# A third PSUM bank for the first pass of the attention, in the units that have bank 7 to spare

## The chip, the cores and the metric

The kernel runs on one core of a Trainium2 chip. The metric is the time of one execution on the device in microseconds (us). The core's engines are TensorE (PE in the profile; its weight loads are PEld), VectorE (DVE), ScalarE (ACT), GpSimd (POOL) and SyncE (SP, which issues most DMAs). They run their own instruction streams in order and wait for each other by semaphores. Matmuls write to PSUM, which has eight banks of 512 float32 in each of 128 partitions.

## What is computed

Two things are added to the input `x` (2 rows of 1024 tokens, 128 features), both from its layer norm: a transformer of four layers, and a mixture of experts (8 experts, 2 for each token) on all 2048 tokens. What matters here is the attention of the four layers: 16 heads of 8 features, causal, with ALiBi.

```python
def mha(x, mask, Wi, bi, Wo, bo):
    ...
    scores = jnp.einsum('bhqd,bhkd->bhqk', q, k) / math.sqrt(HD)
    scores = scores + mask[None]
    attn = jax.nn.softmax(scores, axis=-1)
    out = jnp.einsum('bhqk,bhkd->bhqd', attn, v)
    out = out.transpose(0, 2, 1, 3).reshape(B, T, D)
    return out @ Wo.T + bo
...
for i in range(L):
    xn = layer_norm(x, ln1_w[i], ln1_b[i])
    x = x + mha(xn, mask, in_proj_w[i], in_proj_b[i], out_proj_w[i], out_proj_b[i])
    xn = layer_norm(x, ln2_w[i], ln2_b[i])
    h = jax.nn.gelu(xn @ ffn1_w[i].T + ffn1_b[i], approximate=False)
    x = x + (h @ ffn2_w[i].T + ffn2_b[i])
return layer_norm(x, final_w, final_b)
```

## The kernel before

**Units and phases.** The attention of one row in one layer is cut into four units of four heads. Four units are a phase; a phase handles the attention of one row while projections, FFN and experts of the other row are worked in between. There are eight phases, 32 units: phase "first" (units 0 to 3), then three times "odd" and "even" in a loop over the layers (units 4 to 27, two jumps back), then "last" (units 28 to 31). The loop's body is written once and run three times; all other code is written out.

**Two passes.** The softmax needs each query's maximum. The first pass (`p1_step` on TensorE, `maximum` on VectorE) forms the scores of unit U + 1, 40 steps of up to 512 columns, and takes their row maxima. It has banks 5 and 6 of PSUM in turn: step k writes bank `5 + k % 2` and so waits until the maximum of step k - 2 is taken (`s_p1m`). The steps run over eight query tiles; after step 11 (query tiles 0 to 3) and after step 39 VectorE reduces the maxima to `negm`, one half of the queries each. GpSimd splits `negm` in three bf16 parts (`max_parts`, lines 601 to 608), TensorE turns them (`turn`, line 879) into bank 7, ScalarE copies them out (`turn_out`, line 766, counted by `s_taken`), and DMAs put them into the query operand. The second pass of unit U (`p2_pair`, line 984) then forms scores with the maximum subtracted, ScalarE takes the exponential (`exps`, line 797) from banks 0 to 3, and `p2_values` (line 1002) multiplies with the values into bank 4. A pair of step c waits for the exponential of step c - 2.

**Order.** Nothing is scheduled by a tool: each engine's order is written out by a table, `PLANS`. A unit has 24 slots (one `p2_pair` each) and 48 half slots; `pace` says how many first-pass steps are issued in each half slot; `contents` says in which slot a piece of other work is issued that goes through bank 7, the one bank for all of it: turns of maxima, layer norm transposes, projections (q, k, v), FFN pieces (h, y), the attention's output projection. Such a piece waits until the piece before it is out of the bank (`taken`), so all are numbered in one order (`base + n`).

**Units without other work.** In six units `contents` has nothing but turns: the first and third of "first" (units 0 and 2), the third of "even" (10, 18 and 26) and the third of "last" (30). There bank 7 stands empty between its two or three turns.

Of the kernel before, what the change touches and what calls it, by code (L numbers as in the profile page):

```python
# [33 lines left out]
ALU = mybir.AluOpType  # L34
ACT = mybir.ActivationFunctionType
AXX = mybir.AxisListType.X
# [3 lines left out]
P = 128  # L40
# [6 lines left out]
ROWS = 64  # L47
# [10 lines left out]
def first_pass():  # L58

    steps = []  # L60
    for i in range(TB):
        for c in range(1 + i // 4):
# [7 lines left out]
P1N = len(P1_STEPS)  # L70
P1L = sum(i < TB // 2 for i, *_ in P1_STEPS)
HALVES = 48
PLANS = {
    "first": dict(
        pace=("011111011111011111011111011111011101021111011111",
              "011111011111011112011110011111010111111111011021",
              "011111011111011112001111011111011111101111101111",
              "011101111001111100013101000043011111110111101111"),
        contents=(
# [62 lines left out]
def kind_of(b, f, q):  # L142

    return "first" if f is None else "last" if q is None else ("even", "odd")[b]


def steps_at(b, f, q, j, k):

    if j == 3 and q is None:
        return ()  # L150
    pace = [int(n) for n in PLANS[kind_of(b, f, q)]["pace"][j]]
    return tuple(range(sum(pace[:k]), sum(pace[:k + 1])))


P2_JOBS = [(qh, kt, max(512 * qh, P * kt), 512 * (qh + 1) - max(512 * qh, P * kt))
# [3 lines left out]
SLOTS = 2 * JOBN  # L159
# [41 lines left out]
def chunks_of(b, f, q):  # L201

    if f is None:
        return (3,)
    if q is None:
        return (0, 1)
    return (0, 1, 2, 3) if b == 1 else (0, 1, 3)
# [16 lines left out]
def build(nc, x, cA, rA, cB, moe1, moe2, router_w, rb, fin, ident, identb, iota, m1, m2, route, kcon, qcon, out):  # L224
    with ExitStack() as ctx:
# [642 lines left out]
        def _(pe):  # L868
# [84 lines left out]
                                         wA[:, 2 * D:3 * D], start=True, stop=True)  # L953
                last.then_inc(S["s_full"], 1)

            def p1_step(U, par, kb, nth, k, first=False):
                i, j, c, n, heads = P1_STEPS[k]
                if k == 0:
                    pe.wait_ge(c_ldl[par], 32 * (nth + 1))
                if k == P1L:  # L960
                    pe.wait_ge(c_ldr[par], 32 * (nth + 1))
                if k >= 2 or not first:
                    pe.wait_ge(S["s_p1m"], P1N * U + k - 1)
                r = slice(ROWS * j, ROWS * j + ROWS)
                diagonal = 512 * c + n == P * (i + 1)
                for e, a in enumerate(heads):
                    last = pe.matmul(PS[:, 5 + k % 2, n * e:n * e + n], Qop[r, par, a, P * i:P * i + P],  # L967
                                     Kop[r, kb, a, 512 * c:512 * c + n], start=True, stop=not diagonal)
                    if diagonal:
                        for side in range(2):  # L970
                            at = n * e + n - P + ROWS * side
                            last = pe.matmul(PS[:, 5 + k % 2, at:at + ROWS], mk1[r, side, :], idb[r, r],  # L972
                                             start=False, stop=side == 1)
                last.then_inc(S["s_p1"], 1)

# [31 lines left out]
            def phase(p, b, f, q, base, contents):  # L1007

                row = 1 - b
                g0 = gelus_before(b, f)  # L1010
                done = chunks_of(b, f, q)
                for j in range(PH):
                    U, par, nth = PH * p + j, j % 2, 2 * p + j // 2
                    for s in range(SLOTS):
                        for k in steps_at(b, f, q, j, 2 * s):
                            p1_step(U + 1, 1 - par, (j + 1) % 4, nth + par, k)
                        p2_pair(U, par, j, nth, s)
                        for n, (spots, kind, which) in enumerate(contents):
                            if SLOTS * j + s in spots:
                                if kind[:4] == "turn" and which == 1:  # L1020
                                    turn(base + n, U, par, 1)
                                if kind[:4] == "turn" and which == 0:
# [15 lines left out]
                                        if spots[t] == SLOTS * j + s:  # L1038
                                            y_piece(base + n, which, g0 + done.index(which), group_of(which, b, f), t)
                        for k in steps_at(b, f, q, j, 2 * s + 1):  # L1040
                            p1_step(U + 1, 1 - par, (j + 1) % 4, nth + par, k)
                        if s == 0 and not (f is None and j == 0):
                            p2_values(U - 1, 1 - par, JOBN - 1)
                        if s % 2 == 1 and s >= 3:
# [55 lines left out]
        def _(dve):  # L1100
# [109 lines left out]
                    dve.tensor_tensor(o, o, other, op).then_inc(S["s_fin"], 1)  # L1210
                    dve.wait_ge(S["s_fin"], 3 * (2 * row + c) + k + 1)

            def maximum(U, par, k):
                i, j, c, n, heads = P1_STEPS[k]
                dve.wait_ge(S["s_p1"], P1N * U + k + 1)
                dve.tensor_reduce(mx[:, par, i, 2 * heads[0] + j:2 * heads[-1] + j + 1:2, c],  # L1216
                                  PS[:, 5 + k % 2, 0:n * len(heads)].rearrange("p (h n) -> p h n", n=n), AXX, ALU.max)\
                    .then_inc(S["s_p1m"], 1)
                if k == P1L - 1 or k == P1N - 1:

                    tiles = slice(0, 4) if k == P1L - 1 else slice(4, 8)
                    dve.wait_ge(S["s_p1m"], P1N * U + k + 1)
                    dve.tensor_reduce(negm[:, par, tiles, :], mx[:, par, tiles, :, :], AXX, ALU.max, negate=True)\  # L1223
                        .then_inc(S["s_negm"], 1)
# [16 lines left out]
            def phase(p, b, f, q, base, contents):  # L1241
                row = 1 - b
                at = PLANS[kind_of(b, f, q)]
                for now in range(4 * HALVES):
                    j, k = now // HALVES, now % HALVES
                    U, par = PH * p + j, j % 2
                    for step in steps_at(b, f, q, j, k):
                        maximum(U + 1, 1 - par, step)
                    for n, (_, kind, which, away) in enumerate(at["contents"]):
                        if away == now and not (kind == "h" and CHUNKS[which[0]][0] == "X"):  # L1250
                            out_of_bank(base + n, kind, which, group_of(which, b, f) if kind == "y" else 0, 4 * p, b, row)
# [231 lines left out]
```

## Time and profile before

| what | value |
|---|---|
| median of 3 runs | 1548.06 us (1546.43 to 1549.83) |
| the profiled execution | 1548.17 us |
| its span in the profile | 1546.4 us |
| TensorE busy | 1272.3 us, 82% of the span |
| VectorE busy | 997.0 us, 64% |
| ScalarE busy | 873.0 us, 56% |
| GpSimd busy | 379.2 us, 25% |
| mean granted TensorE clock | 0.921 of full |

The span is the time from the first to the last instruction of the program in the profile; the execution's own time is a little longer. "Busy" is the time in which an engine has an instruction of its own under way. Matmuls are pipelined and their ends are modelled, so a busy TensorE is not one at its peak. All times below are counted from the start of the span.

### The profile page before, as it was taken

The page shows a single profiled execution, that of the slowest core. Times are in us where ns is not written, and L with a number is a line of the kernel's source. Part 1 is how long each engine was busy: PE and PEld are TensorE (multiplying, and loading weights), DVE is VectorE, ACT ScalarE, POOL GpSimd, SP SyncE. Part 2 cuts the span into 40 slices and gives each one's busy share as a digit, 9 for nine tenths or more (in the row PEclk, how much of TensorE's full clock was granted, in tenths as well). Part 3 has the DMA queues.
Part 4 walks back from the last instruction along what each step waited for, and adds up shares of the span by engine and source line. Part 5 has one row for each costly group of instructions (what it writes and reads, how often), then busy time and mean ns, then how long its engine had stood idle before and what let it go on. Part 6 is the DMA issues. An engine that isn't in the chain of part 4 may idle for free.

```text
span 1546.4 us, 35310 instructions
## 1 busy us (share of the span) xinstructions
PE 1272.3 (82%) x12316; PEld 647.1 (42%) x12316; DVE 997.0 (64%) x2120; ACT 873.0 (56%) x1107; POOL 379.2 (25%) x569
## 2 busy tenths in 40 slices
PE   3688788899888887889888897889988898976854
PEld 2333344345444443444444443444544444433323
DVE  5787666666666775666665776657666676745724
ACT  2056556666566664656655665566565666653740
POOL 4044503132031201222122110312203210424501
PEclk9589889999999998999998999999998999988986
DMA  8212414123230312313232131303313041201010
GB/s 247 65 45 86 173 38 128 31 73 116 73 117 19 117 50 65 111 33 115 80 103 66 59 107 54 112 18 114 108 58 97 20 140 36 88 30 48 18 48 15
DMA packets 108919, 120.64 MB, mean 78 GB/s; under 512 B 12097, under 2 KB 95169, under 8 KB 108737
## 3 DMA queue, kind: packets, MB, share of 16 engines
q1 hardware_dynamic: 100288, 90.38, 18.7%
q0 software_dynamic: 8448, 27.88, 6.0%
q8 instruction: 109, 1.79, 0.5%
q14 instruction: 74, 0.60, 0.1%
HBM read 78.63 MB, written 40.89 MB: 77 GB/s over the span
## 4 chain that ended last, share of the span: by engine, by line
PE 52%; DVE 15%; issue 14%; POOL 10%; ACT 6%; DMA 1%; POOLq 0%; DVEq 0%; ACTq 0%; SPq 0%
PE PS L1002 13%; PE PS L967 12%; DVE mx L1216 10%; PE PS L984 5%; PE PS L924 4%; PE PS L927 3%; PE PS L907 3%; PE PS L911 3%; ACT PR L797 2%; POOL xs L614 2%; POOL both L641 2%; PE PS L948 2%; PE PS L972 2%; PE PS L990 2%; PE PS L952 1%
## 5 line engine op out<-in xcount | busy, mean ns | idle before, releaser
L1216 DVE TENSOR_REDUCE mx<-PS 128x1 f32<-128x512 f32 (+3 forms) x1280 | 768.3, 633 | 351.2 <-PE PS L972 231.2
L797 ACT ACTIVATE PR<-PS 128x1024 f32<-128x1024 f32 (+3 forms) x768 | 607.4, 810 | 499.2 <-PE PS L990 311.4
L967 PE MATMUL PS<-Kop,Qop 64*128 64x512 bf16 (+3 forms) x1536 | 438.4, 346 | 140.1 <-DVE mx L1216 135.8
L984 PE MATMUL PS<-Qop,Kop 64*128 64x512 bf16 (+3 forms) x1536 | 349.0, 338 | 16.3 <-ACT PR L797 8.4
L1002 PE MATMUL PS<-PR,vbuf 128*32 128x512 f32 (+3 forms) x3072 | 342.4, 519 | 0.6 <-ACT PR L797 0.4
L967 PEld LDWEIGHTS PS<-Kop,Qop 64*128 64x128 bf16 x1536 | 130.9, 94 | 467.8 <-DVE mx L1216 371.4
L972 PE MATMUL PS<-idb,mk 64*128 64x64 bf16 x2048 | 192.0, 195 | 0.0
L972 PEld LDWEIGHTS PS<-idb,mk 64*128 64x128 bf16 x2048 | 163.4, 98 | 45.1 <-issue 7.2
L990 PE MATMUL PS<-idb,mk 64*128 64x64 bf16 x2048 | 168.3, 194 | 4.7 <-issue 4.7
L601 POOL CAST mp<-negm 128x16 bf16<-128x16 f32 x64 | 14.9, 234 | 555.2 <-DVE negm L1223 555.2
L990 PEld LDWEIGHTS PS<-idb,mk 64*128 64x128 bf16 x2048 | 136.3, 97 | 33.7 <-issue 8.3
L984 PEld LDWEIGHTS PS<-Qop,Kop 64*128 64x128 bf16 x1536 | 106.0, 95 | 104.7 <-ACT PR L797 58.0
L572 POOL TENSOR_TENSOR rstd<-ve,mhalf 128x4 f32<-128x4 f32 x40 | 41.1, 1027 | 240.7 <-DVE ve L1118 240.4
L1002 PEld LDWEIGHTS PS<-PR,vbuf 128*32 128x32 f32 x3072 | 61.6, 109 | 64.9 <-issue 34.6
L907 PE MATMUL PS<-xnT,wF 128*128 128x512 f32 x128 | 76.0, 687 | 11.9 <-ACT xnT L757 9.3
L924 PE MATMUL PS<-wF,hb 128*128 128x128 f32 x512 | 73.2, 294 | 4.5 <-ACT hb L779 2.9
L924 PEld LDWEIGHTS PS<-wF,hb 128*128 128x128 f32 x512 | 64.1, 200 | 13.3 <-issue 6.6
L577 POOL TENSOR_TENSOR x<-x,parts 128x1024 f32<-128x1024 f32 x16 | 34.1, 2128 | 131.1 <-ACT parts L784 131.1
L779 ACT ACTIVATE hb<-hb 128x2048 f32<-128x2048 f32 x26 | 49.7, 1910 | 18.9 <-DVE hb L1138 12.5
L927 PE MATMUL PS<-w2G,hb 128*128 128x128 f32 x320 | 54.0, 322 | 0.4 <-issue 0.4
L590 POOL TENSOR_TENSOR xr<-xr,wR 128x512 f32<-128x512 f32 x28 | 35.6, 1271 | 76.4 <-DVE xc L1130 76.4
L766 ACT ACTIVATE mrow<-PS 12x512 bf16<-12x512 bf16 x64 | 36.8, 575 | 27.5 <-PE PS L879 27.0
(104 smaller groups left out, 1117.3 us busy)
## 6 DMA issues: line engine op xcount, KB each, us to landing
Qop<-qst SPq DMA_DIRECT2D x64, 256.0 KB, 2.8
Kop<-kst SPq DMA_DIRECT2D x64, 256.0 KB, 3.3
kst<-parts SPq DMA_DIRECT2D x32, 256.0 KB, 2.9
qst<-parts SPq DMA_DIRECT2D x16, 384.0 KB, 2.5
kst<-parts SPq DMA_DIRECT2D x32, 128.0 KB, 2.5
qst<-parts SPq DMA_DIRECT2D x16, 256.0 KB, 2.7
Qop<-mrow SPq DMA_DIRECT2D x256, 3.0 KB
onum<-osb SPq DMA_DIRECT2D x256, 16.0 KB
```

The source lines that it names most:

```text
L779: act.activation(hb[:, HBUF[chunk], :, :], hb[:, HBUF[chunk], :, :], ACT.Gelu).then_inc(S["s_gelu"], 1)
L797: act.activation(PR[:, c % 4, :, 0:n], PS[:, 2 * (c % 2):2 * (c % 2) + 2, 0:n], ACT.Exp)\
L907: last = pe.matmul(PS[:, bank, :], wF[:, P * f:P * f + P], xnT[:, row, 512 * c:512 * c + 512], start=True, stop=True)
L911: last = pe.matmul(PS[:, bank, P * m:P * m + P], w1G[:, f, P * m:P * m + P], xGT[:, P * f:P * f + P], start=True, stop=True)
L924: last = pe.matmul(PS[:, bank, P * j:P * j + P], hb[:, HBUF[k], m, P * j:P * j + P], wF[:, F + P * m:F + P * m + P], start=(m == 0), stop= ...
L927: last = pe.matmul(PS[:, bank, P * j:P * j + P], hb[:, HBUF[k], j, P * m:P * m + P], w2G[:, j, P * m:P * m + P], start=(m == 0), stop=(m = ...
L967: last = pe.matmul(PS[:, 5 + k % 2, n * e:n * e + n], Qop[r, par, a, P * i:P * i + P], Kop[r, kb, a, 512 * c:512 * c + n], start=True, sto ...
L972: last = pe.matmul(PS[:, 5 + k % 2, at:at + ROWS], mk1[r, side, :], idb[r, r], start=False, stop=side == 1)
L984: last = pe.matmul(PS[:, 2 * (c % 2) + j, 0:n], Kop[r, kb, a, P * kt:P * kt + P], Qop[r, par, a, q0:q0 + n], start=True, stop=not DIAG[t])
L990: last = pe.matmul(PS[:, 2 * (c % 2) + j, ROWS * side:ROWS * side + ROWS], mk2[r, side, :], idb[r, r], start=False, stop=side == 1)
L1002: last = pe.matmul(PS[32 * h:32 * h + 32, 4, q0 - 512 * qh:512], vbuf[:, par, kt, h, :], PR[:, 2 * (t % 2) + h // 2, h % 2, 0:n], start=t ...
L1216: dve.tensor_reduce(mx[:, par, i, 2 * heads[0] + j:2 * heads[-1] + j + 1:2, c], PS[:, 5 + k % 2, 0:n * len(heads)].rearrange("p (h n) -> p ...
```

## The change

A new function `banks_at` gives for each first-pass step of a unit its bank, and the step that used this bank last. In all units but the six it answers as before (banks 5 and 6 in turn). In the six, a step may go to bank 7 if no turn stands near it: a turn at half slot `at` keeps steps of half slots `at - 3` to `at + 4` out of bank 7, and the last two steps of a pass stay in 5 and 6. Of the free banks it takes the one that was used longest ago. A step in bank 7 waits for `s_taken` too, so that the last turn is out of the bank, and a turn waits for the maximum of the last step in bank 7.

```diff
+BARE = {"first": (0, 2), "even": (2,), "last": (2,)}
+
+def banks_at(b, f, q, j):
+    kind = kind_of(b, f, q)
+    if j not in BARE.get(kind, ()):
+        return [(5 + k % 2, k - 2) for k in range(P1N)]
+    halves = [k for k in range(HALVES) for _ in steps_at(b, f, q, j, k)]
+    used = [2 * (s - SLOTS * j) for spots, _, _, _ in PLANS[kind]["contents"] for s in spots]
+    last, banks = {5: -2, 6: -1, 7: -3}, []
+    for k, half in enumerate(halves):
+        free = all(at + 5 <= half or half + 4 <= at for at in used)
+        bank = 5 + k % 2 if k >= P1N - 2 else min((5, 6, 7) if free else (5, 6), key=last.get)
+        banks.append((bank, last[bank]))
+        last[bank] = k
+    return banks
...
-            def p1_step(U, par, kb, nth, k, first=False):
+            def p1_step(U, par, kb, nth, k, first=False, where=None):
                 i, j, c, n, heads = P1_STEPS[k]
+                bank, same = (5 + k % 2, k - 2) if where is None else where
...
-                if k >= 2 or not first:
-                    pe.wait_ge(S["s_p1m"], P1N * U + k - 1)
+                if same > -3 and (k >= 2 or not first):
+                    pe.wait_ge(S["s_p1m"], P1N * U + same + 1)
...
+                seventh = None
+
+                def first_pass_step(U, par, j, nth, k, emitted):
+                    where = banks_at(b, f, q, j)[k]
+                    if where[0] == 7:
+                        taken(emitted)
+                    p1_step(U + 1, 1 - par, (j + 1) % 4, nth + par, k, where=where)
+                    return P1N * (U + 1) + k + 1 if where[0] == 7 else seventh
...
                         for n, (spots, kind, which) in enumerate(contents):
                             if SLOTS * j + s in spots:
+                                if seventh is not None:
+                                    pe.wait_ge(S["s_p1m"], seventh)
+                                    seventh = None
...
-                        maximum(U + 1, 1 - par, step)
+                        maximum(U + 1, 1 - par, step, banks_at(b, f, q, j)[step][0])
```

No matmul, maximum or DMA is added, removed or put in another place. What differs in an engine's order is only what TensorE's steps wait for. On TensorE in unit 0, behind the first turn, this stood before (`Kop,Qop` is a first-pass step, `Qop,Kop` a pair of the second pass, `PR,vbuf` the values; the waits are in brackets):

```order
L967 MATMUL PS<-Kop,Qop 128x384 [waits s_p1m]
L972 MATMUL PS<-idb,mk 128x64 x2
L967 MATMUL PS<-Kop,Qop 128x512 [waits s_p1m]
L972 MATMUL PS<-idb,mk 128x64 x2
L984 MATMUL PS<-Qop,Kop 128x256 [waits s_exp]
L984 MATMUL PS<-Qop,Kop 128x256
L990 MATMUL PS<-idb,mk 128x64 x4
L967 MATMUL PS<-Kop,Qop 128x512 [waits s_p1m]
L972 MATMUL PS<-idb,mk 128x64 x2
L1002 MATMUL PS<-PR,vbuf 32x384 [waits s_exp]
```

In the changed program the same place reads so (its line numbers are 20 higher here):

```order
L987 MATMUL PS<-Kop,Qop 128x384 [waits s_taken]
L992 MATMUL PS<-idb,mk 128x64 x2
L987 MATMUL PS<-Kop,Qop 128x512 [waits s_p1m]
L992 MATMUL PS<-idb,mk 128x64 x2
L1004 MATMUL PS<-Qop,Kop 128x256 [waits s_exp]
L1004 MATMUL PS<-Qop,Kop 128x256
L1010 MATMUL PS<-idb,mk 128x64 x4
L987 MATMUL PS<-Kop,Qop 128x512 [waits s_p1m]
L992 MATMUL PS<-idb,mk 128x64 x2
L1022 MATMUL PS<-PR,vbuf 32x384 [waits s_exp]
```

Its first row is step 7, the first in bank 7: it waits for the copy of the turn instead of a maximum. The steps behind it still wait for `s_p1m`, but for a value that is one lower, the maximum of step k - 3.

## Rows read from the trace of the kernel before

**Rows 1.** The page, part 1: busy us (share of the span) xinstructions.
```profile
PE 1272.3 (82%) x12316; PEld 647.1 (42%) x12316; DVE 997.0 (64%) x2120; ACT 873.0 (56%) x1107; POOL 379.2 (25%) x569
```

**Rows 2.** Windows: unit 10, sum and mean of all six; us, busy by engine, clock.
```profile
523.30:554.10 30.80, 27.39 (x339) 12.51 (x336) 23.80 (x43) 21.54 (x30) 6.23 (x11) 1.00 0.40 130
...
sum 194.00, PE 165.04 PEld 74.65 DVE 145.94 ACT 127.29 POOL 78.41; mean PE 27.51 PEld 12.44 DVE 24.32 ACT 21.21 POOL 13.07
```

**Rows 3.** TensorE's waits, units 0, 2, 10, 30: us in total, times, longest.
```profile
PE PS L967 <- DVE mx L1216: 4.3, 8, 1.3
...
PE PS L967 <- DVE mx L1216: 3.6, 8, 0.8
...
PE PS L967 <- DVE mx L1216: 3.0, 7, 0.7
...
PE PS L967 <- DVE mx L1216: 3.5, 10, 0.6
```

**Rows 4.** TensorE's waits in 529:550, 172:179, 183:192, 91:100 and 103:113.
```profile
PE PS L967 <- DVE mx L1216: 2.1, 5, 0.7
...
PE PS L967 <- DVE mx L1216: 1.3, 3, 0.8
...
PE PS L967 <- DVE mx L1216: 1.5, 3, 0.6
...
PE PS L967 <- DVE mx L1216: 1.1, 2, 0.7
...
PE PS L967 <- DVE mx L1216: 1.6, 4, 0.5
```

**Rows 5.** Timeline, unit 10: start us, us, what, xcount [idle before <-releaser].
```profile
534.83 2.12 ACT L797 ACTIVATE PR<-PS 128x1024 f32<-128x1024 f32 x2 [1.00 <-PE PS L990]
...
535.23 0.39 PE L967 MATMUL PS<-Kop,Qop 64*128 64x512 bf16 x1 [0.25 <-DVE mx L1216]
...
537.00 0.38 PE L984 MATMUL PS<-Qop,Kop 64*128 64x384 bf16 x2
```

**Rows 6.** Timeline of VectorE, unit 10.
```profile
533.84 2.85 DVE L1216 TENSOR_REDUCE mx<-PS 128x1 f32<-128x512 f32 x5
536.95 2.22 DVE L1216 TENSOR_REDUCE mx<-PS 128x2 f32<-128x256 f32 x4 [0.25 <-PE PS L972]
```

**Rows 7.** Timeline, unit 2, VectorE and TensorE.
```profile
177.69 2.20 DVE L1216 TENSOR_REDUCE mx<-PS 128x2 f32<-128x256 f32 x4 [0.25 <-PE PS L972]
...
178.52 0.39 PE L967 MATMUL PS<-Kop,Qop 64*128 64x512 bf16 x1
```

**Rows 8.** VectorE late in unit 0: a row of its timeline, a window.
```profile
107.43 2.20 DVE L1216 TENSOR_REDUCE mx<-PS 128x1 f32<-128x384 f32 x4 [0.32 <-PE PS L972]
...
107.40:116.90 9.50, 7.28 (x68) 2.35 (x66) 8.77 (x25) 6.12 (x8) 4.16 (x4) 1.00 0.23 77
```

**Rows 9.** Timeline, unit 30 to the turn of unit 31, GpSimd and TensorE.
```profile
1440.38 0.21 POOL L601 CAST mp<-negm 128x16 bf16<-128x16 f32 x1 [8.27 <-DVE negm L1223]
...
1461.09 0.68 POOL L601 CAST mp<-negm 128x16 bf16<-128x16 f32 x1
...
1464.01 0.39 PE L879 MATMUL PS<-idb,mp 128*12 128x128 bf16 x4 [1.73 <-POOL mp L608]
```

**Rows 10.** Timeline, unit 0, ScalarE's copy of the turn and step 7.
```profile
90.38 0.57 ACT L766 ACTIVATE mrow<-PS 12x512 bf16<-12x512 bf16 x1
...
90.86 0.32 PE L967 MATMUL PS<-Kop,Qop 64*128 64x384 bf16 x1
```

**Rows 11.** Timeline of TensorE at both jumps back; DMA queues in 595:604 (packets, MB).
```profile
598.68 0.61 PE L984 MATMUL PS<-Qop,Kop 64*128 64x512 bf16 x2 [3.45 <-issue]
601.36 0.29 PE L990 MATMUL PS<-idb,mk 64*128 64x64 bf16 x4 [2.07 <-issue]
...
966.88 0.29 PE L990 MATMUL PS<-idb,mk 64*128 64x64 bf16 x4 [2.59 <-issue]
...
q8 instruction: 3, 0.05, 2.0%
```

More of the change, by code:

```diff
@@ L966, in p1_step @@
                 for e, a in enumerate(heads):
-                    last = pe.matmul(PS[:, 5 + k % 2, n * e:n * e + n], Qop[r, par, a, P * i:P * i + P],
+                    last = pe.matmul(PS[:, bank, n * e:n * e + n], Qop[r, par, a, P * i:P * i + P],
                                      Kop[r, kb, a, 512 * c:512 * c + n], start=True, stop=not diagonal)
@@ L971, in p1_step @@
                             at = n * e + n - P + ROWS * side
-                            last = pe.matmul(PS[:, 5 + k % 2, at:at + ROWS], mk1[r, side, :], idb[r, r],
+                            last = pe.matmul(PS[:, bank, at:at + ROWS], mk1[r, side, :], idb[r, r],
                                              start=False, stop=side == 1)
@@ L1015, in phase @@
                         for k in steps_at(b, f, q, j, 2 * s):
-                            p1_step(U + 1, 1 - par, (j + 1) % 4, nth + par, k)
+                            seventh = first_pass_step(U, par, j, nth, k, base + sum(e[0][0] < SLOTS * j + s for e in contents))
                         p2_pair(U, par, j, nth, s)
@@ L1040, in phase @@
                         for k in steps_at(b, f, q, j, 2 * s + 1):
-                            p1_step(U + 1, 1 - par, (j + 1) % 4, nth + par, k)
+                            seventh = first_pass_step(U, par, j, nth, k, base + sum(e[0][0] <= SLOTS * j + s for e in contents))
                         if s == 0 and not (f is None and j == 0):
@@ L1211, in final, with maximum @@
                     dve.wait_ge(S["s_fin"], 3 * (2 * row + c) + k + 1)
-            def maximum(U, par, k):
+            def maximum(U, par, k, bank=None):
                 i, j, c, n, heads = P1_STEPS[k]
+                bank = 5 + k % 2 if bank is None else bank
                 dve.wait_ge(S["s_p1"], P1N * U + k + 1)
                 dve.tensor_reduce(mx[:, par, i, 2 * heads[0] + j:2 * heads[-1] + j + 1:2, c],
-                                  PS[:, 5 + k % 2, 0:n * len(heads)].rearrange("p (h n) -> p h n", n=n), AXX, ALU.max)\
+                                  PS[:, bank, 0:n * len(heads)].rearrange("p (h n) -> p h n", n=n), AXX, ALU.max)\
                     .then_inc(S["s_p1m"], 1)
```

## The prediction

> **What bounds the kernel now.** I read the page's first part, then busy time and waits by unit, then the timeline. A unit is a group of four heads; the kernel runs 32 of them (0 to 31), and while unit U's attention runs, the engines also do the first pass (scores and row maxima) of unit U + 1. TensorE is the busiest engine, 82% of the span [rows 1].
>
> The change touches the first pass in six units only: 0 and 2, then 10, 18 and 26 (the third unit of each even phase), and 30. The reader should see two things in their windows [rows 2]. First, they are short, 194 us in sum, 32 us each in the mean, and TensorE is busy 27.5 us of that, more than VectorE (24.3) or ScalarE (21.2). So TensorE's waits there are worth time, but no engine is far behind it. Units 18 and 26 repeat unit 10 within 0.1 us. Second, with two banks step k of the pass can't start before the maximum of step k - 2 is taken, and TensorE's waits for these maxima (VectorE's line 1216) are small [rows 3]: 4.3, 3.6, 3.0 and 3.5 us in units 0, 2, 10 and 30, so 4.3 + 3.6 + 3 x 3.0 + 3.5 = 20.4 us in the six. That is the ceiling of what a third bank can remove, 1.3% of the time.
>
> **The waits that can go.** Around each turn of the maxima the change stays with two banks. Working banks_at out for each plan gives 9, 9, 8 and 10 steps in bank 7 (units 0, 2, each even one, 30). Where three banks rotate, a step waits for the maximum of step k - 3, or an older one.
>
> Unit 10: between 529 and 550, where all steps that would wait have the longer distance, lie five waits and 2.1 us [rows 4]; the other 0.9 us of the 3.0 are at steps that keep two banks, and stay. From the 2.1 I take off what the other engines can't follow. ScalarE's two exponentials from 534.83 run back to back until 536.95, and TensorE's next pair of score matmuls starts 0.05 us later, at 537.00 [rows 5]: it waits for the exponential, so most of the 0.25 us that would go at 535.23 is taken back there. VectorE works from 533.84 to 536.69, pauses 0.25 us, and works through to 539.17 [rows 6]; the next step that keeps two banks meets the end of that run earlier than before, about 0.1 us. I take 1.8 us; the ends are nothing and 2.1. Three such units: 5.4 us.
>
> Unit 2: waits of 1.3 us before 179 and 1.5 us after 183 have the longer distance [rows 4]. But in between, step 19, which keeps two banks, starts at 178.52, just when two of the four maxima in VectorE's run from 177.69 to 179.89 can be done [rows 7]; VectorE's only pause before that run is 0.25 us, so the 1.3 shrinks to about 0.3. Of the 1.5 behind it ScalarE takes back some 0.2, as in unit 10. I take 1.6, between 0.3 and 2.8.
>
> Unit 0: 1.1 us before 100 and 1.6 us from 103 to 113 [rows 4]. But from 107.4 to 116.9 VectorE is busy 8.8 of 9.5 us, with a pause of 0.32 us just ahead of that stretch [rows 8]: layer norm statistics stand between the maxima, and TensorE follows VectorE to the unit's end. So the unit ends earlier only by what was gained before, cut by a step like unit 2's, and by that pause. I take 1.0, between 0.3 and 2.7.
>
> Unit 30: nothing. GpSimd gets the first half's maxima of unit 31 at 1440.38, then combines the expert outputs, and reaches the second half's at 1461.09 without having waited for anyone; TensorE already waits 1.73 us for that at the turn [rows 9]. The half that starts this run is complete with step 11 of 40, and by the hand-worked table none of its waits goes. TensorE gains up to 2.6 us in the rest of unit 30 (the 3.5 less 0.9 that stay or come before) and gives it back at the turn. For the longer idle there I add a loss of 0.3 us, between 0 and the 1.73 that it is now.
>
> The units between have no change, and the shift passes through them: GpSimd's 6.9 us run that TensorE waits for in unit 2 starts from unit 1's projections, so it moves with unit 0. Sum of this part: 5.4 + 1.6 + 1.0 - 0.3 = **7.7 us**.
>
> **What it adds.** The steps in bank 7 also wait for the copy of the last turn (s_taken). In unit 0 ScalarE's copy runs from 90.38 to 90.95 and step 7 started at 90.86 [rows 10], so it is held by some 0.15 us; the same holds in unit 2, and both are in the values above. In the other places the copy ends well ahead. A turn now waits for the last maximum out of bank 7, at least five half slots older, cost nothing; if VectorE were that late, it is one maximum, 0.7 us a turn. In the built program TensorE gets 16 more wait instructions ahead of the loop, 3 in it, 8 behind it: 16 + 3 x 3 + 8 = 33 executed. In unit 10 it issues 339 + 336 instructions in 30.8 us [rows 2], 0.046 us each, so 33 cost 0 to 1.5 us; since nearly all are met and TensorE's queue runs ahead of its array, I take 0.5.
>
> **What it moves.** Those 16 instructions move the loop's first instruction. At the jump back TensorE stops twice [rows 11]: 3.45 us, then it runs two matmuls, then 2.07 us more, both "issue", that is, no semaphore; at the second jump the second stop is 2.59 us. In that stretch its instruction queue q8 brings three packets, 0.05 MB, so 16 KB each [rows 11]. I read the second stop as the wait for the code's next 16 KB block: the jump lands some 7 instructions before a block's end. With 16 instructions more in front, the loop's start falls some 9 behind that border, and the block that the jump brings is nearly whole. Both second stops go: 2.07 + 2.59 = **4.7 us**; the other end is 0. By the Trainium skill, Runtime: NRT & Kernel Launch, section Instruction fetch mechanics, code comes in 16 KiB blocks of 256 instructions, read ahead in sequence, and a jump out of the window waits for its block; the trace agrees with the size and with one wait a jump, and the second wait then is a matter of where the target lies.
>
> **Sum.** 7.7 + 4.7 - 0.5 = 11.9 us. The profiled execution took 1548.17 us (a span of 1546.4 and 1.8 around it), 0.1 from the median of 1548.06: 1548.2 - 11.9 = **1536.3 us**.
>
> **Rivals.**
> (a) The stops at the jumps stay, because the border is not where I put it: only the waits go, 1548.2 - 7.2 = 1541.0. For it: the place rests on one pattern, seen twice.
> (b) The pass is paced by VectorE and ScalarE after all; the jumps gain, and of the waits 1 us: 1548.2 - 4.7 - 1 + 0.5 = 1543.0. For it: VectorE's long runs [rows 6, 8].
> (c) Neither comes, and each engine takes back what another gives: 1548. The change then doesn't do what it says. Against it: VectorE's pauses [rows 6, 7] are waits for TensorE, so both were waiting for each other.
> (d) Slower: the copy of the turn holds TensorE. ScalarE works in order, and the copy stands behind an exponential of 1.06 us [rows 5]. If the first bank-7 step after each of the 12 turns were held for both, 1.06 + 0.57, that is 12 x 1.6 = 19 us against 12 gained: 1555. It decides from 1.0 us a turn. Against it: the 0.1 us of [rows 10].
> (e) More: the ends of matmuls are modelled, and waits that the matmul rows hide go too, so that all 20.4 us of [rows 3] vanish: 1548.2 - 20.4 - 4.7 + 0.5 = 1523.6. Against it: the two-bank steps and GpSimd's run in unit 30.
>
> **Chances.** Forecast 0.50 (1532 to 1540), (a) 0.20, (b) 0.10, (c) 0.10, (d) 0.06, (e) 0.04. A measurement of this kernel can tell about 0.2%, 3 us, from no change. Below 1545 is faster: 0.50 + 0.20 + 0.10 + 0.04 = 0.84; (c) is the same, 0.10; (d) is slower, 0.06. The range leaves out (c), (d) and (e): 1531 to 1545, whose upper end also holds (b) with all its waits kept and the added instructions at 1.5.
>
> **What would show it.** In the profile after: units 10, 18 and 26 some 29.0 us long instead of 30.8, with about 1 us of waits for maxima; unit 30 shorter, but TensorE's wait for GpSimd in unit 31 near 4 us instead of 1.73; at each jump one stop of some 3.5 us, not two. Units as long as before with TensorE waiting for exponentials instead would make (b) right; a second stop still there, (a); TensorE's bank-7 steps waiting for the copy of the turn, (d).

## The result, and the profile after

The changed kernel took 1529.91 us (median of 4 runs, 1525.88 to 1537.32), the kernel before beside it 1548.94 (4 runs, 1546.43 to 1553.40): a ratio of 0.9872, with an interval of 0.9835 to 0.9910. It is faster, by 19 us (1.3%) where 11.9 were forecast; the median lies 1.1 us below the predicted range. The profiled execution took 1525.88 us, with a span of 1524.1. Six more runs of the same kernel, in the experiments below, lay higher: a median of 1535.88. All ten have a mean of 1533.9. Here and below a median is of all runs, while ratios and their intervals leave out two slow runs, over 1.5% above the fastest of their kernel (1567.67 us of the kernel before, 1564.38 in experiment 5).

The first part of the profile's page shows TensorE 15.0 us less busy than in [rows 1], with the same number of instructions:

```profile
PE 1257.3 (82%) x12316; PEld 637.8 (42%) x12316; DVE 994.9 (65%) x2120; ACT 871.6 (57%) x1107; POOL 379.7 (25%) x569
```

The span is 22.3 us shorter, so only some 7 of these are idle time of TensorE. The rest is the same matmuls in less time. Some 2.6 of the 15.0 us lie in the six touched units; what is left lies elsewhere, and is a matter of TensorE's granted clock (0.921 in the mean before, 0.929 after), which comes up again below.

Windows of units 0, 2, 10, 30 and 31 (start and end, length, busy time of PE, PEld, DVE, ACT, POOL, then the granted clock, the DMA share and GB/s):

```profile
84.23:114.89 30.66, 27.72 (x323) 12.80 (x323) 26.55 (x58) 19.80 (x27) 20.26 (x29) 0.89 0.19 61
154.68:191.00 36.32, 27.77 (x332) 11.94 (x328) 23.09 (x42) 21.31 (x29) 20.85 (x28) 0.86 0.53 182
522.13:551.04 28.91, 27.18 (x340) 12.63 (x338) 23.41 (x43) 21.64 (x30) 6.22 (x11) 1.00 0.43 138
...
1407.14:1435.06 27.92, 25.46 (x333) 11.55 (x330) 23.22 (x44) 20.57 (x28) 17.42 (x23) 1.00 0.09 26
1435.06:1461.70 26.64, 19.16 (x216) 6.25 (x212) 7.84 (x9) 19.43 (x27) 5.78 (x7) 0.87 0.11 30
```

Before, these five were 31.95, 39.22, 30.82, 30.38 and 23.44 us long (measured, as here, from a unit's first pair of score matmuls to the next unit's, and unit 31 up to its last eight matmuls with the values). Units 18 and 26 are 28.91 too. TensorE's waits in units 0, 2, 10 and 30, which answer to [rows 3], and the one in unit 31:

```profile
PE PS L987 <- DVE mx L1250: 2.3, 3, 1.9
...
PE PS L987 <- DVE mx L1250: 1.1, 3, 0.6
...
PE PS L987 <- DVE mx L1250: 1.4, 4, 0.4
...
PE PS L987 <- DVE mx L1250: 2.1, 6, 0.7
...
PE PS L898 <- issue: 4.5, 1, 4.5
```

The last is called "issue" since the profile found no semaphore event for it. The timeline of GpSimd and TensorE shows what it is, beside [rows 9]:

```profile
1417.50 0.21 POOL L620 CAST mp<-negm 128x16 bf16<-128x16 f32 x1 [8.10 <-DVE negm L1257]
...
1440.86 0.66 POOL L627 TENSOR_TENSOR mp<-mres,mp 128x16 bf16<-128x16 f32 x1
...
1441.62 0.58 PE L898 MATMUL PS<-idb,mp 128*12 128x128 bf16 x4 [4.52 <-issue]
```

GpSimd's last part of the maxima ends at 1441.52 and the turn starts 0.10 us later: TensorE waited 4.52 us for GpSimd, where it was 1.73.

The timeline of TensorE at both jumps back, to the first turn behind each, beside [rows 11]:

```profile
595.19 0.61 PE L1004 MATMUL PS<-Qop,Kop 64*128 64x512 bf16 x2 [4.21 <-issue]
595.59 0.32 PE L1010 MATMUL PS<-idb,mk 64*128 64x64 bf16 x4
...
601.23 0.39 PE L898 MATMUL PS<-idb,mp 128*12 128x128 bf16 x4
...
948.34 0.61 PE L1004 MATMUL PS<-Qop,Kop 64*128 64x512 bf16 x2 [3.57 <-issue]
948.74 0.32 PE L1010 MATMUL PS<-idb,mk 64*128 64x64 bf16 x4
...
953.71 0.39 PE L898 MATMUL PS<-idb,mp 128*12 128x128 bf16 x4
```

And the DMA queue that brings its code, in 591:601 (packets, MB, share):

```profile
q8 instruction: 2, 0.03, 1.5%
```

One stop at each jump, not two, and two packets of code instead of three. The kernel before has these rows at the same turns, and at the first stop of its second jump:

```profile
606.88 0.39 PE L879 MATMUL PS<-idb,mp 128*12 128x128 bf16 x4
...
963.68 0.61 PE L984 MATMUL PS<-Qop,Kop 64*128 64x512 bf16 x2 [3.63 <-issue]
...
972.26 0.39 PE L879 MATMUL PS<-idb,mp 128*12 128x128 bf16 x4
```

From the end of the last matmul ahead of the jump (the start of the row with the stop, less the stop) to this turn it was 606.88 - (598.68 - 3.45) = 11.65 us, and 12.21 at the second jump; it is 601.23 - (595.19 - 4.21) = 10.25, and 8.95. The two jumps give 4.66 us.

The places that the change touches add up, in the two profiled executions: unit 0 1.29, unit 2 2.90, units 10, 18 and 26 3 x 1.91 = 5.73, jumps 4.66, units 30 and 31 together a loss of 0.74: **13.8 us**. The spans differ by 22.3. The other 8.5 lie where the code is as it was, 4.6 of them in the 21 units that hold neither a change nor a jump.

**Where the rest is.** Unit 14 has no change. Its windows in the kernel before and after, and then the stretches in the middle of it:

```profile
704.20:746.86 42.66, 39.00 (x400) 22.13 (x397) 27.35 (x48) 26.80 (x33) 10.36 (x16) 0.92 0.33 103
...
722.48:725.53 3.05, 1.99 (x23) 1.27 (x15) 1.67 (x3) 1.91 (x2) 0.19 (x1) 1.00 0.00 1
725.53:728.58 3.05, 2.21 (x25) 0.99 (x26) 2.54 (x5) 3.02 (x4) 1.99 (x2) 0.91 0.24 76
728.58:731.62 3.04, 3.04 (x29) 1.45 (x27) 2.14 (x4) 1.67 (x4) 1.89 (x2) 0.50 0.68 186
731.62:734.67 3.05, 3.05 (x14) 2.48 (x12) 0.69 (x1) 1.02 (x1) 0.00 (x0) 0.50 0.32 103
```

```profile
697.69:737.73 40.04, 36.37 (x400) 20.35 (x397) 27.25 (x48) 26.53 (x33) 10.36 (x16) 1.00 0.36 111
...
717.71:720.57 2.86, 1.66 (x14) 0.50 (x16) 2.73 (x5) 2.48 (x2) 1.23 (x2) 1.00 0.02 6
720.57:723.43 2.86, 2.23 (x35) 1.38 (x37) 2.40 (x4) 2.85 (x6) 1.98 (x3) 1.00 0.48 123
723.43:726.29 2.86, 2.86 (x28) 1.98 (x20) 1.46 (x3) 1.06 (x2) 0.86 (x1) 1.00 0.81 246
```

In both, TensorE is busy about two thirds of the time for some 6 us, around the middle of the unit (4.20 of 6.10 us before, 3.89 of 5.72 after). In the kernel before, its granted clock then fell to half (1.2 instead of 2.4 GHz) for about 7 us; after, it stayed, and the unit is 2.6 us shorter. Is that the change? In the next run of the changed kernel, unit 14 took 42.50 us at 0.92 again (experiment 1). So the same code differs by this much from one execution to another.

### The profile page after: what moved, and what is told of

Read it like the earlier page. It is cut to its first block, busy times and chain, and to the rows that moved or that the text cites. A ratio compares the mean times of both kernels' runs of the same rounds, so it can differ in the third digit from the quotient of the medians.

```text
span 1524.1 us, 35343 instructions
## 1 busy us (share of the span) xinstructions
PE 1257.3 (82%) x12316; PEld 637.8 (42%) x12316; DVE 994.9 (65%) x2120; ACT 871.6 (57%) x1107; POOL 379.7 (25%) x569
## 4 chain that ended last, share of the span: by engine, by line
PE 50%; DVE 15%; issue 15%; POOL 9%; ACT 6%; DMA 2%; SPq 1%; POOLq 0%; DVEq 0%; ACTq 0%
PE PS L1022 13%; PE PS L987 11%; DVE mx L1250 10%; PE PS L1004 5%; PE PS L943 4%; PE PS L926 3%; PE PS L930 3%; PE PS L946 3%; ACT PR L816 2%; PE PS L967 2%; POOL xs L633 2%; POOL both L660 2%; PE PS L992 2%; PE PS L1010 1%; POOL w2G L653 1%
## 5 line engine op out<-in xcount | busy, mean ns | idle before, releaser
L1004 PE MATMUL PS<-Qop,Kop 64*128 64x512 bf16 (+3 forms) x1536 | 345.3, 337 | 16.5 <-issue 7.8
L926 PE MATMUL PS<-xnT,wF 128*128 128x512 f32 x128 | 74.6, 675 | 11.9 <-ACT xnT L776 9.3
L1163 DVE TENSOR_SCALAR xc<-xr,mv,rstd 128x128 f32<-128x128 f32 x128 | 37.6, 341 | 21.5 <-POOL rstd L591 21.5
```

The costliest lines, as they stand in the source:

```text
L926: last = pe.matmul(PS[:, bank, :], wF[:, P * f:P * f + P], xnT[:, row, 512 * c:512 * c + 512], start=True, stop=True)
L1004: last = pe.matmul(PS[:, 2 * (c % 2) + j, 0:n], Kop[r, kb, a, P * kt:P * kt + P], Qop[r, par, a, q0:q0 + n], start=True, stop=not DIAG[t])
```

## The experiments

The theory after the first result: the change is worth what its places show, some 9 us from the third bank and some 5 from the loop's place in memory, and what is above that is the clock of single executions. There are two rivals: nearly all of the gain is the loop's place, or the third bank does more than its units show.

**1. The changed kernel once more.** No edit.

> The changed kernel once more, unaltered, for a second trace and a closer interval. Theory A: what the change does is in nine places: units 0, 2, 10, 18, 26, 30 with 31 (together about -9.4 us in the first trace after) and the units behind the two jumps back (12 and 20, together about -7.7 us); the other -5 us of the first trace lie in units without any change and are chance in TensorE's granted clock. Then this trace repeats the nine places within 0.3 us a unit (the jump units within 2), the other units differ again in sum and in place, and the time is about 1532, ratio 0.989. Theory B: the other units gain by the change too; then they repeat their -5 us unit by unit, and the ratio is 0.986 or less.

1535.88 us (6 runs, 1530.12 to 1543.44; before beside it 1547.69, 15 runs, 1542.98 to 1560.50), ratio 0.9909 (0.9877 to 0.9941). The windows of unit 14 and, after its second jump, of unit 20:

```profile
696.74:739.24 42.50, 38.84 (x401) 21.97 (x398) 27.36 (x48) 26.79 (x33) 10.36 (x16) 0.92 0.34 104
...
953.95:1010.39 56.44, 49.18 (x398) 24.13 (x398) 33.50 (x83) 31.19 (x40) 14.62 (x19) 0.86 0.30 84
```

The touched units nearly repeat: 31.01, 36.46, three times 28.9, and 54.49 for 30 and 31. There is one stop a jump, 4.19 and 3.52. The other units don't repeat: unit 14 has lost its 2.5 us again, and unit 20, 50.73 in the first trace, is 56.44 at a clock of 0.86, where within 2 us was expected. The span is 11.1 below before, not 22.3. The places of the change give 12.0 us in this trace, so all the rest together gives nothing (-0.9), where it gave 8.5. These six runs lie 5.3 us above the first four in the mean, with a standard error of 3.2: most likely the first four were a lucky draw.

**2. The loop's place alone.** The kernel before, with 16 semaphore increments on TensorE ahead of its loop; the third bank is not there.

```diff
+            for _ in range(16):
+                pe.sem_inc(passed, 1)
```

> The kernel before, two banks everywhere, with 16 instructions more in TensorE's stream (increments of a semaphore that nothing waits for, at its start, where it waits for constants): the loop's first instruction moves as far as in the change. Theory A (the place of the loop in its 16 KB code block makes the second stop at a jump): one stop at each jump instead of two, 4.7 to 7.7 us less than before, 1541 to 1543.5; no change in the six units. Rival (the second stop went because the third bank moved other work): both stops stay, 1548, same.

1538.0 us (6 runs, 1535.9 to 1542.16), ratio 0.9924 (0.9898 to 0.9950). Its timeline of TensorE at the first jump:

```profile
601.03 0.61 PE L986 MATMUL PS<-Qop,Kop 64*128 64x512 bf16 x2 [3.97 <-issue]
601.42 0.32 PE L992 MATMUL PS<-idb,mk 64*128 64x64 bf16 x4
```

The code's queue brings two packets in 597:606. The second stop and the third packet are gone with nothing but 16 instructions in front. To the first turn it is 9.86 and 8.90 us, against 11.65 and 12.21: 5.1 us in the trace. The timed runs say more, 11.8 us (7.7 to 15.8), and their median lies below the 1541 to 1543.5 that were expected. The units that aren't touched have the same sum in both traces (21 units without a jump or a change, 983.5 and 983.9), so this profile doesn't show where the excess is.

**3. The banks without the loop's place.** The changed kernel, with 240 such increments at the same place: with the 16 of the change that makes 256, the number of instructions that the prediction gives for one block of code, so the loop's start should stand in a block where it stood before.

```diff
+            for _ in range(240):
+                pe.sem_inc(passed, 1)
```

> The changed kernel with 240 instructions more at TensorE's start, so that with its own 16 the loop lies a whole block of 256 further than before, at the old place in its block. Theory A: the second stop is back at both jumps, and what is left is the third bank alone, 9 us below before, 1539; slower than the changed kernel by 5 to 8. Rival: one stop at each jump, as in the changed kernel, about 1530 to 1532.

1560.59 us (7 runs, 1557.12 to 1562.84), ratio 1.0058 (1.0028 to 1.0087), slower than before, since the increments weren't hidden. Its timeline of TensorE at the first jump:

```profile
616.15 0.61 PE L1006 MATMUL PS<-Qop,Kop 64*128 64x512 bf16 x2 [3.55 <-issue]
618.89 0.29 PE L1012 MATMUL PS<-idb,mk 64*128 64x64 bf16 x4 [2.14 <-issue]
```

The DMA queues in 612:622, as above:

```profile
q8 instruction: 3, 0.05, 1.8%
```

The window of unit 0:

```profile
105.46:136.13 30.67, 27.49 (x323) 12.68 (x322) 26.55 (x58) 19.81 (x27) 20.27 (x29) 0.89 0.20 62
```

Unit 0 starts at 105.46 instead of 84.38: the 240 cost 21.1 us, 0.088 each, an error of the design. Less that, it is 1539.5. Both stops and the third packet are back at both jumps (second: 3.55 and 2.14), as they should be if the code comes in blocks of 256 instructions. The six units have the lengths of the changed kernel (30.67, 36.31, 28.91). So the two parts are independent of each other.

**4. The even phases alone.** `BARE = {"even": (2,)}`, units 10, 18 and 26.

> The third bank in units 10, 18 and 26 alone; nothing is added ahead of the loop, so the loop lies where it lay. Theory A: each of the three units 1.9 us shorter, 28.9 instead of 30.8, both stops stay at each jump, 5.8 us below before: 1542.3. Rival (the units' gain is given back behind them, and the time comes from elsewhere): the three units are shorter, but the units behind them longer, 1546 to 1548.

1543.02 us (9 runs, 1539.41 to 1546.21), ratio 0.9960 (0.9939 to 0.9982), that is 2.8 to 9.4 us. Its timeline of TensorE at the first jump:

```profile
602.31 0.61 PE L1004 MATMUL PS<-Qop,Kop 64*128 64x512 bf16 x2 [3.47 <-issue]
605.02 0.29 PE L1010 MATMUL PS<-idb,mk 64*128 64x64 bf16 x4 [2.10 <-issue]
```

Both stops stay. Units 10, 18 and 26 are 28.91 us long: the lengths give 5.7 us, the timed runs 6.2. What the units gain is not given back behind them.

**5. The last phase alone.** `BARE = {"last": (2,)}`, unit 30.

> The third bank in unit 30 alone; nothing added ahead of the loop. Theory A (GpSimd's run of combining the expert outputs sets when unit 31's turn comes): unit 30 is 2.5 us shorter (27.9 instead of 30.4), TensorE's wait for GpSimd at the turn grows from 1.73 to about 4.2, unit 31 is 3.2 us longer, in sum 0.7 us slower than before: 1548.5, same. Rival (the gain goes through): 1545 to 1546.

1547.81 us (12 runs; before beside it 1548.27, 22 runs, 1539.81 to 1560.40), ratio 0.9991 (0.9958 to 1.0025). Windows of units 30 and 31:

```profile
1432.12:1460.03 27.91, 25.46 (x332) 11.56 (x329) 23.20 (x44) 20.57 (x28) 17.41 (x23) 1.00 0.09 25
1460.03:1486.71 26.68, 19.20 (x216) 6.26 (x212) 7.15 (x8) 19.43 (x27) 5.78 (x7) 0.87 0.11 30
```

Unit 30 gives 2.47 us and unit 31 takes 3.24 back. A loss of 0.8 can't be told by the timed runs. In the traces, the way from the start of unit 30 to the turn in unit 31 is 34.47 to 34.50 us in all six with the third bank in unit 30 and the combination in its old place, and 34.14 to 34.17 in all five without that bank.

**6. All but the last phase.** `BARE = {"first": (0, 2), "even": (2,)}`.

> The changed kernel without the third bank in unit 30. Theory A: 0.7 us faster than the changed kernel, which these rounds can't tell from none; in the trace units 30 and 31 together 53.8 us as before the change, instead of 54.5, the other eight places as in the changed kernel. Rival: 2.5 us slower than the changed kernel, since unit 30's share is lost.

1535.83 us (6 runs, 1529.23 to 1540.72), ratio 0.9900 (0.9857 to 0.9942), the same as experiment 1 within the intervals. Its units 30 and 31 are 30.38 and 24.75 us, 55.13 together where the changed kernel has 54.56 and the one before 53.82, so in this execution nothing was saved by leaving unit 30 alone. TensorE waits 1.3 us there for the DMA of the turned maxima (`Qop<-mrow`), and 1.4 in experiment 4, a wait that the kernel before doesn't have in its trace. So the loss of 0.74 is not one that every execution shows.

**7. The experts' combination later.** The changed kernel, with GpSimd's combination behind the second half of unit 31's maxima instead of ahead of it (and the last layer norm's slot moved to suit it).

```diff
-                    if q is None and j == 2:
+                    if q is None and j == 3:
                         wait_apart(pool, S["c_both"], 16 * RANKS)
```

> The changed kernel, with GpSimd combining the expert outputs behind the maxima of unit 31's second half instead of ahead of them, and VectorE's final layer norm parts of row 0 two slots before the end of unit 31 instead of early in it. Theory A: the turn in unit 31 no longer waits for GpSimd, unit 30 keeps its 27.9 us and unit 31 falls from 26.6 to some 22, so 4 us faster than the changed kernel (and the waits of 1.73 that the kernel before had are gone too). Rival: the combining then ends too late for the final part, and the tail behind unit 31 grows by what is gained.

1533.82 us (11 runs, 1524.67 to 1546.89), ratio 0.9906 (0.9867 to 0.9944): no difference from the changed kernel that shows, where 4 us were expected. TensorE's waits in unit 31, all of them:

```profile
PE PS L1004 <- ACT PR L816: 3.2, 7, 0.7
PE PS L1004 <- DMA Qop<-mrow: 1.7, 1, 1.7
```

It no longer waits for GpSimd at the turn. Of the 4.5 us some are now waits for the turned maxima's DMA (1.7) and for exponentials (3.2, and 2.3 in the changed kernel). The unit takes 24.00 us, 2.6 less (22 were expected), and what follows it to the end of the span 1.1 more (63.5 instead of 62.4).

**8 and 9. No jump.** The changed kernel with its loop over the layers written out on all five engines, twice (6 runs each), and the kernel before treated alike.

```diff
-            with pe.Fori(0, L - 1, 1) as l:
+            for l in range(L - 1):
```

> The changed kernel with the loop over the layers written out three times on every engine: no jump back at all. Theory A (the stop at a jump is the wait for its code block): the remaining stops of 4.2 and 3.6 us go as well, and the lower clock behind them, units 12 and 20 fall from about 51 to 46, 8 to 12 us faster than the changed kernel, about 1523. Rival: the code stream then needs as many blocks in a row as before, and stops turn up elsewhere, same as the changed kernel.

> The kernel before, with its loop over the layers written out three times, so that nothing jumps back on any engine. Against the changed kernel written out (1516.3 us) it holds the effect of the third bank apart from that of the loop's place in memory. Theory A (the third bank is worth the 9 us that the units' lengths show in the traces with a loop, and the loop's place the rest): 1525 us, between 1522 and 1529, with units 10, 18 and 26 some 30.8 us long, unit 2 some 39.2. Theory B (the gain is nearly all of the loop's place and of TensorE's clock behind it, and what the third bank saves is given back later): 1516, within 3. Theory C (the third bank is worth all of the 15 us that the timed runs show, since less waiting also brings a higher clock in other units): 1531, between 1529 and 1535.

> The changed kernel with the loop written out, once more, beside the kernel before with the loop written out, on the same chip and against the same runs: 1516 us, within 4. Both theories expect the same here; it is the other side of the difference that tells them apart.

| kernel, loop written out | us | ratio |
|---|---|---|
| before | 1526.65 (1521.08 to 1530.28) | 0.9841 (0.9801 to 0.9882) |
| changed | 1516.26 (1513.84 to 1521.38) | 0.9790 (0.9748 to 0.9832) |
| changed, again | 1522.99 (1516.84 to 1533.05) | 0.9810 (0.9769 to 0.9852) |

The means are 1526.5 (before) and 1517.2 and 1523.5 (changed). The first row and the last were run on one chip, the middle one on another. On the one chip the third bank is worth 3.0 us without any jump, with a standard error of 2.8, which can't be told from nothing; with all 12 runs of the changed kernel it is 6.2 with 2.1, but then two chips are mixed. Either way it is less than the 15 us of theory C, which asked for 1529 to 1535. The lengths of the touched units say 8.8 in the last trace (unit 10: 30.81 and 28.90; unit 30: 30.37 and 27.92), and 6.7 in the middle one, whose unit 2 took 38.75. The last row lies outside the 1516 within 4 that were expected of it. Unit 12 in the three traces, in the order of the table:

```profile
594.11:644.12 50.01, 42.55 (x403) 20.58 (x400) 34.01 (x85) 31.33 (x40) 15.52 (x23) 1.00 0.34 101
```

```profile
588.85:637.61 48.76, 42.52 (x403) 20.57 (x400) 33.92 (x85) 31.32 (x40) 15.49 (x23) 1.00 0.36 104
```

```profile
597.76:652.84 55.08, 46.74 (x402) 23.23 (x400) 34.00 (x85) 31.31 (x40) 15.48 (x23) 0.91 0.31 91
```

There is no stop in any of them; from the last matmul of unit 11 to the first turn it is 4.1 us. Unit 12 is not down to the 46 us that were expected. The second and the third row are the same code, 6.3 us apart, with TensorE's clock at 1.00 and 0.91. Stops and half clock at the two jumps are together worth 11.65 + 12.21 - 2 x 4.1 = 15.7 us of the kernel before; its timed runs gain 24.7 (18.3 to 30.9).

**10. Both.** The changed kernel with the loop written out and the combination later.

> The changed kernel with the loop written out and the experts' combination behind the second half of unit 31's maxima. If the 2.6 us that unit 31 was shorter with the combination later reach the end, less the 0.8 that the tail was longer: 1514.5 us, between 1511 and 1517, with unit 31 some 24 us long. If they don't: 1516.

1512.67 us (6 runs, 1508.75 to 1515.96), ratio 0.9754 (0.9715 to 0.9792), the fastest that was run. Unit 31 is 23.66 us long where the other two traces of the written-out kernel have 26.49 and 26.48, and what follows it takes 1.4 more (63.6 and 62.2). So its trace accounts for 1.4 us; its runs lie 10.8 us below those of the row "changed, again" on the same chip (standard error 2.7), and no stretch was found that holds the difference.

The time from the last matmul ahead of a jump to the first turn behind it, worked out as above in every trace with a loop:

```
two stops:  before 11.65 12.21   exp. 3 12.60 12.69   exp. 4 11.78 12.58   exp. 5 11.75 13.52   mean 12.3
one stop:   after  10.25  8.95   exp. 1 10.78  9.87   exp. 2  9.86  8.90   exp. 6 10.38  9.85   exp. 7 10.22 10.51   mean 10.0
no jump:    4.1 in all four
```

The two groups don't overlap. A second stop is worth 2.4 us, 4.8 for both jumps.

## Why the prediction was right, and where it failed

Two steps of the prediction failed. It took all units without a change to last as long as in the one trace, which put TensorE's clock there at nothing without a reason; the code that the change doesn't touch gave 8.5 us in the first profiled execution and -0.9 in the second. And its term for unit 2, 1.6 us, was too small: 2.90 were measured, more than the end that it gave. The other terms lie, in the first trace, within the ends that it gave them.

**Units 10, 18 and 26: right.** 1.8 us each were taken, "the ends are nothing and 2.1"; these units are 28.90 to 28.92 us long in every trace with a third bank there, 1.9 less. TensorE's waits for maxima fell from 3.0 to 1.4 us in unit 10. The two exponentials at 534.83, feared to take back 0.25 us, don't: TensorE waits for no exponential in the unit any more, and ScalarE waits for TensorE. VectorE works through in unit 10:

```profile
532.09 4.93 DVE L1250 TENSOR_REDUCE mx<-PS 128x1 f32<-128x512 f32 x9
```

**The jumps: right in mechanism, and in size as far as the traces go.** "Both second stops go: 2.07 + 2.59 = 4.7 us". The jumps gave 4.66 in the first trace, 3.2 in the second, and 4.8 in the mean of all. Experiments 2 and 3 show the cause: 16 instructions ahead of the loop do it without the third bank, and 240 more undo it with it. By the Trainium skill, Runtime: NRT & Kernel Launch, section Instruction fetch mechanics, a jump out of the window waits for its block; the traces agree with one wait for each jump (3.45 to 4.21 us), and they show the second, of 2.07 to 2.69 us, to come and go with the place of the target.

**Unit 2: a term that was too small.** "I take 1.6, between 0.3 and 2.8"; it is 2.90 (2.76 in experiment 1). Ahead of the unit's last turn 0.3 were taken. The reason given was that step 19, which keeps two banks, is held by VectorE's run, whose "only pause before that run is 0.25 us", so that the 1.3 us of waits ahead of it would shrink to about 0.3 of gain. The run was misread. In the kernel before the first half of it reads:

```profile
174.85 2.59 DVE L1216 TENSOR_REDUCE mx<-PS 128x1 f32<-128x512 f32 x4
```

The second half are the four in [rows 7], two of them with half as many columns. After, the same eight maxima read:

```profile
173.19 4.33 DVE L1250 TENSOR_REDUCE mx<-PS 128x1 f32<-128x512 f32 x8
```

They take 4.33 us with no pause, where it was 174.85 to 179.89, 5.04. Of these 0.71 us of pauses only 0.25 is printed; the rest is inside two rows that look solid. So VectorE wasn't the limit, and the step went ahead: to the turn, the unit gained 0.74 us (from its start 24.42 before, 23.68 after).

The larger part of the miss lies behind the turn, where 1.3 were taken and 2.16 came. The clock is 1.00 there before and after. The waits for maxima fell from 2.4 to 0.9 us, and TensorE's busy time for 130 matmuls fell as well, from 12.35 to 11.48: so the rows of busy matmuls held waiting too, which the prediction counted as work. This stretch took 14.80 us in all five traces without the third bank in unit 2, and 12.62 to 12.64 in seven of the eight with it (13.62 in experiment 8). Ahead of the turn the clock differs, and unit 2 as a whole spreads from 38.96 to 42.65 us without the bank and from 36.30 to 38.75 with it.

Unit 0, where 1.0 was taken, gave 1.29 and 0.94; over all traces it spreads from 31.82 to 32.98 us without the bank and from 29.31 to 31.84 with it.

**Units 30 and 31: right in mechanism, too small.** Nothing for unit 30 and a loss of 0.3 were taken, with TensorE's wait for GpSimd "near 4 us": it is 4.52, and from unit 30's start to the turn it is 34.48 instead of 34.16 us, 0.32 later. That isn't the longer idle, for which the loss was put in. GpSimd's run begins 0.17 us sooner after the unit's start (10.36 instead of 10.53; steps 9 to 11 do have the longer distance, other than the prediction says), but it lasts 24.02 us instead of 23.58. Its last two additions take 1.50 us each, where they took 1.27 and 1.28. VectorE's part of the final layer norm (`xc<-xc,finw`) now starts 0.54 us ahead of the first of these, at 1435.00; before, it started at 1460.17, within the second. So it is in all six traces with the third bank in unit 30 and the combination in its old place, and in all five without that bank. The last addition, after and before:

```profile
1437.21 1.50 POOL L673 TENSOR_TENSOR xin<-xin,both 128x512 f32<-128x512 f32 x1 [0.18 <-POOL xin L673]
```

```profile
1459.87 1.28 POOL L654 TENSOR_TENSOR xin<-xin,both 128x512 f32<-128x512 f32 x1 [0.18 <-POOL xin L654]
```

The other 0.4 come behind the turn. After the longer idle TensorE starts at a lower clock: the four matmuls of the turn take 0.58 us where [rows 9] had 0.39, and the granted clock of unit 31 is 0.87, not 0.93.

**The additions: right that they cost little.** No 0.5 us for 33 waits shows anywhere. No step of the first pass is listed in the trace as waiting for the copy of a turn. In unit 0 it reads, with step 7 behind it, beside [rows 10]:

```profile
89.54 0.57 ACT L785 ACTIVATE mrow<-PS 12x512 bf16<-12x512 bf16 x1
...
90.17 0.33 PE L987 MATMUL PS<-Kop,Qop 64*128 64x384 bf16 x1
```

Step 7 starts 0.06 us after the copy's end, with no idle time in front. With that, rival (d) falls; (a) falls by the single stops, (b) and (c) by the units' lengths. Of (e) a part is true: in unit 2 the gain of 2.90 is more than the 2.5 us by which the waits fell, and in unit 30 TensorE's busy time fell from 26.76 to 25.46 us at a clock of 1.00.

**The sum and the range.** The terms missed by 1.3 (unit 2), 0.3 (unit 0), 0.3 (the even units) and 0.5 (the added waits) on one side and 0.4 (unit 31) on the other: 13.8 where 11.9 were forecast, 1534.4 us, inside the range. The mean of ten runs is 1533.9; that it comes so close is in part luck, since the second trace gives 12.0. What put the first median outside the range is what the sum had no term for. It took every unit without a change to last as long as in the one trace, and they don't: TensorE's clock in them differs from run to run, the 51 runs of the kernel before that are compared here lie between 1539.8 and 1561.5, and the first four runs of the changed one have a median 6 us below that of the next six. The prediction put what a measurement can tell at 3 us. The range was made of the unknown costs alone.

**What stays open.** The kernel before gained in time, with the 16 increments and with its loop written out, more than the traces show at the jumps: 11.8 for 5.1, and 24.7 for 15.7 us. Why is open. Perhaps a shorter stop also spares half-clock stretches later. In units 14 to 17 and 22 to 25, behind each jump, the traces with two stops sum to 184.1 us in the mean of eight, those with one to 182.7 of ten; but they run from 182.2 to 185.0 and from 178.2 to 184.8, so this is not shown.

## What to carry to other kernels

Here a third buffer was worth about the waits that it removed, or up to 1.1 us a unit more, where no other engine was solid. Before calling an engine solid, look at its instructions one by one: a row of the timeline is named by one shape and can hold several, and pauses too short to be printed are inside. A change that adds instructions ahead of a loop moves the loop's start in the code's blocks, and here that was worth 4.8 us at two jumps, beside some 9 us of the change itself by the lengths of its units: try the padding alone, and the loop written out. Where TensorE's granted clock falls in one execution and not in the next, add that spread to the range, and compare the lengths of the touched stretches, not two spans.

## What the runs showed of the hardware

- The same stretch of the same code runs at either clock. Behind the 6.9 us in which TensorE waits for GpSimd in unit 2, its clock is at half in the four traces that were cut so finely, but it comes back at different times. In the written-out kernel (experiment 8) and in the first trace of the changed kernel the time from 15 to 18 us after the unit's start reads:

```profile
170.28:173.28 3.00, 3.00 (x30) 1.13 (x28) 1.81 (x3) 1.19 (x3) 0.47 (x1) 0.50 0.04 9
```

```profile
169.68:172.68 3.00, 2.98 (x50) 1.26 (x46) 2.67 (x5) 1.91 (x5) 0.45 (x1) 1.00 0.04 10
```

  TensorE was busy all the time in both, with 30 and 50 matmuls done. The unit took 38.75 and 36.32 us.
- The two jumps back cost the kernel before 15.7 us, of which 3.45 + 2.07 + 3.63 + 2.59 = 11.7 are stops. The rest is the same work at a lower clock: from the first stop's end to the turn the granted clock is 0.61 in the mean, and 1.00 at the same place with the loop written out.
- 240 semaphore increments in a row on TensorE took 21.1 us, 0.088 us each.
- VectorE and GpSimd held each other up at the end of unit 30. GpSimd's additions of 128x512 took 1.26 to 1.28 us, and 1.50 where VectorE's layer norm part had started ahead of them; VectorE's instructions of that part, 0.69 us each by themselves, took 0.91, 1.65 and 1.63 there. GpSimd's cast of 128x16 ahead of the turn took 0.67 us; in experiment 7, where that part of VectorE comes later, it took 0.21.
